# An RWKV block on one core: the centring of the first state is moved behind the first chunk's mixes

## The reference

```
xn  = layernorm(x);  sx = previous token of xn - xn
xxx = tanh((xn + sx*maa_x) @ maa_w1)                 # 5 parts of 32
x5[g] = xn + sx * (maa_stack[g] + xxx[g] @ maa_w2[g])  # 5 mixes: k w v r g
w = exp(-exp(time_decay + tanh(x5[w] @ decay_w1) @ decay_w2))
r, k, v = x5[r] @ Wr.T, x5[k] @ Wk.T, x5[v] @ Wv.T;  g = silu(x5[g] @ Wg.T)
for each token: out = r . (u*k*v + s);  s = k*v + w*s  # 32 heads, state 8x8 each
att = groupnorm(out) * g
x  = x + att @ Wo.T
xn2 = layernorm(x); sx2 = token shift of xn2
x  = x + sigmoid(xr @ Wr2.T) * (square(relu(xk @ Wk2.T)) @ Wv2.T)
```

## Time and profile before

| | |
|---|---|
| median of 3 runs | 509.7 us (507.69, 509.7, 1242.73) |
| the profiled execution | 507.84 us |
| its span | 506.0 us |
| VectorE busy | 467.0 us, 92% of the span |
| TensorE busy with matmuls | 475.6 us, 94% |
| ScalarE busy | 281.4 us, 56% |
| GpSimd busy | 89.6 us, 18% |
| mean granted clock of TensorE | 0.993 |

### The profile page before, as it was taken

How to read it: one execution, slowest core, us unless ns; L and a number is a source line. 1 busy time by engine, 2 the same in 40 slices (tenths; PEclk the granted TensorE clock), 3 DMA queues, 4 the chain that set the end, 5 groups by cost and what they waited for, 6 DMA issues and landing times. The chain is left out here.

```text
span 506.0 us, 6206 instructions
## 1 busy us (share of the span) xinstructions
PE 475.6 (94%) x2172; PEld 277.4 (55%) x2172; DVE 467.0 (92%) x521; ACT 281.4 (56%) x611; POOL 89.6 (18%) x100
## 2 busy tenths in 40 slices
PE   3788899999999999999999999999999999988797
PEld 2564545655446347544556456644655556556476
DVE  3779898999999999999999999999999999998665
ACT  2354666477546834777447764563558463455343
POOL 0101003210610051011401051003130231203020
PEclk9899999999999999999999999999999999999999
DMA  8365685597869576993789664884869477905031
GB/s 272 123 161 114 169 173 104 116 211 162 149 174 230 123 122 157 213 204 63 133 200 223 133 124 111 212 207 81 181 139 211 79 113 178 217 2 114 0 40 34
DMA packets 28136, 73.03 MB, mean 144 GB/s; under 512 B 1737, under 2 KB 20297, under 8 KB 25673
## 3 DMA queue, kind: packets, MB, share of 16 engines
q1 hardware_dynamic: 19720, 54.68, 44.2%
q0 software_dynamic: 8384, 17.96, 21.2%
HBM read 46.28 MB, written 12.19 MB: 116 GB/s over the span
## 5 line engine op out<-in xcount | busy, mean ns | idle before, releaser
L624 DVE TENSOR_TENSOR_SCAN kv<-w_sb,kv 128x512 f32<-128x512 f32 (+2 forms) x144 | 146.9, 1083 | 0.9 <-ACT w_sb L859 0.6
L952 PE MATMUL pa<-x,large_sb 128*128 128x512 f32 (+2 forms) x272 | 115.2, 567 | 4.6 <-DVE x L539 3.9
L952 PEld LDWEIGHTS pa<-x,large_sb 128*128 128x128 f32 x272 | 51.0, 194 | 60.3 <-issue 47.5
L632 DVE TENSOR_TENSOR kv<-kv,r_sb 128x2048 f32<-128x2048 f32 (+2 forms) x36 | 73.5, 2045 | 0.3
L614 DVE TENSOR_TENSOR kv<-vrep,k_sb 128x2016 f32<-128x2016 f32 (+2 forms) x34 | 70.1, 2061 | 1.1 <-PE patt L1124 1.1
L445 POOL COPY kv<-s_sb 128x32 f32<-128x32 f32 (+2 forms) x36 | 30.0, 837 | 157.4 <-PE patt L1124 145.4
L414 POOL DMA_DIRECT2D x<-xn x28 | 28.2, 1008 | 145.9 <-DVE x L530 145.5
L530 DVE SCALAR_TENSOR_TENSOR x<-pb,vec_sb,sx 128x512 f32<-128x512 f32 (+1 forms) x64 | 42.7, 708 | 2.4 <-PE pb L1030 1.4
L1124 PE MATMUL patt<-kv,const_sb 128*32 128x512 f32 (+2 forms) x288 | 33.7, 555 | 0.0
L996 PE MATMUL pb<-th,w_sb 32*128 32x512 f32 (+2 forms) x100 | 33.4, 597 | 0.0
L1164 PE MATMUL pc<-large_sb,att 128*128 128x256 f32 x120 | 28.2, 386 | 2.2 <-DVE att L648 2.2
(11 more groups left out here) (187 smaller groups left out, 806.6 us busy)
## 6 DMA issues: line engine op xcount, KB each, us to landing
vrep<-v_scratch SPq DMA_DIRECT2D x12, 2048.0 KB, 15.7
x<-xn POOLq DMA_DIRECT2D x24, 512.0 KB, 5.7
vrep<-v_scratch SPq DMA_DIRECT2D x4, 1536.0 KB, 12.7
x_tok<-in_x SPq DMA_DIRECT2D x6, 512.0 KB, 10.0
v_scratch<-v_sb SPq DMA_DIRECT2D x12, 256.0 KB
xres<-in_x SPq DMA_DIRECT2D x6, 512.0 KB, 4.5
out<-xres SPq DMA_DIRECT2D x6, 512.0 KB, 10.1
out<-trr POOLq DMA_DIRECT2D x6, 512.0 KB, 9.1
```

The lines of the kernel that those rows point to most:

```text
L624: ins = dve.tensor_tensor_scan(flat, w_sb[:, p, q % HF, 0:nb].rearrange("p b t -> p (b t)"), flat, 0.0, ALU.mult, ALU.add)
L632: dve.tensor_tensor(flat, flat, r_sb[:, p, q % HF:q % HF + 1, 0:n].broadcast_to([P, G4, n]), ALU.mult).then_inc(rs_ready, 1)
L952: ins = pe.matmul(dst[:, m, 0:n], w(a)[:, m * P:(m + 1) * P], src[:, a, :], start=(a == 0), stop=(a == HF - 1))
```

## The change

Two steps change their place in two lists. No instruction is added or removed.

```diff
 DVE_STEPS = """
-    st1.0 nrm1.0 shift.0 cwv.0 cs0.0 mix0.0 mix3.0 mix2.0 mix1.0 a0.0 a1.0 sc0.0 rk.0 mix4.0 shift.1 sc1.0 rs0.0
+    st1.0 nrm1.0 shift.0 cwv.0 mix0.0 mix3.0 mix2.0 mix1.0 cs0.0 a0.0 a1.0 sc0.0 rk.0 mix4.0 shift.1 sc1.0 rs0.0
...
 POOL_STEPS = """
-    rd1.0 ad0.0 ad3.0 s00.0 rd1.1 ad0.1 s01.0 rd1.2 ad1.0 s02.0 s03.0 s00.1 s01.1 ad0.2 ad1.1 ad1.2 rd2.0 ad3.1
+    rd1.0 ad0.0 ad3.0 rd1.1 s00.0 ad0.1 s01.0 rd1.2 ad1.0 s02.0 s03.0 s00.1 s01.1 ad0.2 ad1.1 ad1.2 rd2.0 ad3.1
```

## The result

The changed kernel took 505.6 us in the median of six runs (504.68 to 506.41); the kernel before took 508.9 beside it. The ratio is 0.9944, with a 95% interval of 0.9928 to 0.9961. By it the change is 2.85 us faster (1.98 to 3.66), clear of noise though far under 2%. Two executions of the kernel before that were far out (1242.73 and 564.0 us) are left out of every ratio and mean that follows. The profiled execution took 506.04 us with a span of 504.2, against 507.84 and 506.0: 1.8 us less.

A forecast was written before the change was run, and what follows sets the result against it. VectorE was taken as the bound past some 60 us, the first scan's start carrying the result. The earlier mix0.0 gave 1.05 us, with P0.0 at full clock 1.73, off 507.84: 506.1 us; range 504.6 to 509.2.

The forecast's parts named there:

- mix0.0 moves ahead: First chunk on VectorE: mix0.0 starts at 17.63 us, not 18.68, held only by X01.0's end; 1.05 us earlier.
- The clock: P0.0 on TensorE takes 1.99 us, not 3.53, after a shorter hole; P1.0 then starts 1.73 us earlier.
- rival (a): The clock still falls on P0.0, so the gain is only 1.05 us: 506.8 us; chance 0.23.
- rival (c): The slow stretch near 75 us falls elsewhere and VectorE's 1.07 us hole ending at 84.92 goes: 505.0 us; chance 0.07.
- cs0.0 under the hole's cover: cs0.0, run behind mix1.0 in the hole before a0.0, delays a0.0 by 0.2 us, hidden by the decay's path.
- GpSimd: rd1.1 put ahead of the copy s00.0: no gain by itself, but saves about 2 us the first move would cost.
- Rival (b): The gain is swallowed later by a wait that does not move with the work: 507.8 us; chance 0.10.
- Rival (d): The clock falls once more on TensorE at 26 to 31 us, besides on P0.0: 0.7 us slower, 508.5; chance 0.10.

The follow-up runs named there:

- VectorE's half alone: Kernel before with only cs0.0 moved behind mix1.0 on VectorE, rd1.1 still behind s00.0 on GpSimd; ratio to the kernel before 0.9999 (0.9976 to 1.0022).
- the other order: Changed kernel with the first chunk's mixes in the order mix0 mix2 mix1 mix3; ratio to the kernel before 0.9940 (0.9911 to 0.9968).
- the changed kernel again: Changed kernel rerun unaltered to count its slow stretches; median 506.04 us of 12, ratio to the kernel before 0.9960 (0.9941 to 0.9979).
- the longer centring: Changed kernel with each of cs0.0's two sums made twice, values unchanged; median 508.35 us, ratio to the kernel before 0.9999 (0.9978 to 1.0021).

## Why the prediction was right, point by point

The forecast of 506.1 us stands 0.5 above the median of 505.6, and the 1.73 us of gain beside 1.8 in the profiled pair; against the medians the gain is 2.85 and the forecast 0.6 of it. That 1.73 and 1.80 lie so close is luck: the forecast is 1.05 + 0.68, and the profiled gain is -0.17 + 0.68 + 0.66 + 0.63, whose last term was not in the sum.

*mix0.0 moves ahead, 1.05 us.* The mechanism was right: the 1.82 of waiting and 3.43 of work gave only the part up to X01.0's end. The profiled pair shows 0.68, because X01.0 ended 13.25 us (18.12 - 4.87) behind VectorE's first instruction where the kernel before had 12.88. I took X01.0's end as fixed. In seven profiles mix0.0, where it waits for X01.0, came between 12.45 and 13.74 behind that instruction. Over many executions the term is 1.16 to 1.19, known to 0.6 us at best, and 1.05 fits it.

*The clock.* I chose the full clock for P0.0, and the profiled execution had it, P0.0 at 1.99 us and P1.0 1.17 us earlier. The reason I gave was wrong. I argued from a hole of 2.15 us ahead of W1.0 that "kept the clock", with a granted clock of 1.00. W1.0's four matmuls of 128x256 take 2.05 us there, and CB.0's four of the same form 1.13: **TensorE ran at half speed until 16 to 18 us, though the window's row says 1.00**. (With VectorE's half alone X01.0's matmuls still take 0.63 us each at its end, at 18.7.) There was no full clock to keep. Behind a hole of 1.7 us the clock does fall at times: one third of the executions of the changed kernel have a slow stretch, and of five profiles with it, three (the other order, the changed kernel again and the longer centring) show the fall. So rival (a) was real in kind. Its price, 0.80 us from mix0.0 to the scan (12.57 against 11.77), was in the one such pair of profiles made good by a faster X01.0. That the first profile kept the clock on P0.0 was in part luck.

*The size of the clock term.* 0.68 at the scan is right: 12.43 against 11.75 with nothing but the clock changed. What I left out of the sum is that the kernel before has 1.30 slow stretches in the mean and the profile showed two of them; the second, near 75 us, I kept only as rival (c), at a chance of 0.07. It is absent in the changed kernel's profiles: rival (c) came true beside the forecast, with 0.63 us and not 1.1, since a new hole of 0.77 opened. In the ten profiles the time from the first scan to the end is 474.13 to 474.43 us in the six without a slow stretch behind the scan, 474.89 to 475.49 in the three with the one near 75 us. The step that was mis-sized is the term of the clock: about 1.1 us over many executions (the difference of two uncertain numbers), not 0.68.

*cs0.0 under the hole's cover.* Right. The spreading of v ends at 26.71 (26.33 + 0.38). In the kernel before a0.0 followed that end by 0.14 us (27.50 + 0.38 to 28.02), which gives the 26.85 at which a0.0 starts here: cs0.0 held it back by nothing that can be seen, where 0.2 was forecast. The decay's path leaves 0.64 us to spare (some 0.4 was forecast), and the longer centring showed that what goes beyond it is paid at the scan.

*GpSimd.* Right: no gain by itself (1.0018, 0.9996 to 1.0040), and without it 1.87 us are lost at the scan, "about 2" in the prediction.

*Rival (b), the gain is swallowed.* It did not come: the distance between the profiles is 1.17 at the first scan and grows to 1.8. *Rival (d), slower:* no slow stretch appeared between 26 and 31 us in the changed kernel. It has its like in the kernel with VectorE's half alone, where every execution had at least one; its profile shows it from 32 to 36 us, with a granted clock of 0.57. *The chances* add up to 1.00 before the 0.01 on each side, so they are 0.02 too many.

## What to carry to other kernels

Where two engines' lists meet in one result, moving a step on one of them alone can turn its gain into a wait on the other; look for what else is queued behind the step that consumes the result, as rd1.1 was behind the copy. Before a granted clock is taken as proof, compare the duration of a matmul of the same form and count elsewhere in the trace. When a change is worth under 1%, split the executions by their mean granted clock first: the part at equal clock is the schedule's, the rest is the clock's, and unused matmuls in one hole can test which is which.

## What the runs showed of the hardware that I had not expected

- The granted clock reads 1.00 from the start of the trace, while matmuls run at half speed: 2.05 us for four of 128x256 at 11.92, 1.13 us at 33.01. The matmuls of X01.0 speed up between 16 and 18 us, from 0.63 to 0.37 us each, at a time that differs from run to run; in one of ten profiles they had not yet done so at 18.7 us.
- A hole of 1.68 to 1.70 us behind matmuls of 32 rows lost the clock in some executions of the same kernel and kept it in others (P0.0 3.66 and 1.99 us). In five profiles the fall went with an early speed-up of X01.0.
- Executions of the kernel before with one slow stretch have spans 1.4 us longer than those with none, and those with two another 0.7, though a stretch at half speed for 3.4 us could cost 1.7 by an estimate from its length. Why the later one, near 75 us, is there in the profiles with the first scan at 31.0 to 31.1 us and in none of the others stays open.
- GpSimd's copy of 16 columns took 0.21 us in some places and 0.56 or 0.85 in others (18.82, 19.79 and 45.77 us in the kernel before); both copies together took 0.34 beside the products. It had no part in the result.
